# Row tiles move as 64 and 61 rows, and ScalarE's queue issues 19 of the loads between two graph layers

## The reference

```python
def _mgcn_conv(x, edge_index, edge_type, rel, W_in, W_out, W_loop, b, n):
    src, dst = (edge_index[0], edge_index[1])
    m = x[src] * rel[edge_type]
    m = jnp.concatenate([m[:half] @ W_in, m[half:] @ W_out], 0)
    deg = jax.ops.segment_sum(jnp.ones((e,), x.dtype), dst, num_segments=n)
    norm = 1.0 / jnp.maximum(deg, 1.0)
    agg = jax.ops.segment_sum(m * norm[dst][:, None], dst, num_segments=n)
    return jnp.tanh(agg + x @ W_loop + b)
...
h = emb + res * _mgcn_conv(emb, edge_index, edge_type, rel1, W_in1, W_out1, W_loop1, b1, num_nodes)
h = h + res * _mgcn_conv(h, edge_index, edge_type, rel2, W_in2, W_out2, W_loop2, b2, num_nodes)
return h @ mu_w + mu_b
```

## Time and profile before

| | |
|---|---|
| runs before | 1943.16 us median of 3 (1937.86 to 1951.39) |
| the profiled execution | 1951.01 us |
| its span in the trace | 1949.2 us |
| PE busy | 1757.6 us, 90% of the span |
| POOL, DVE, ACT busy | 1300.5, 1223.5, 628.7 us |
| granted TensorE clock, mean | 0.97 |
| queue of SyncE (q1) | 93124 packets, 126.68 MB, 20.2% of 16 engines |
| queue of ScalarE (q10) | 28352 packets, 22.24 MB, 4.2% |

### The profile page before, as it was taken

The page is one execution under the profiler, slowest core; times in us unless marked ns, Lnnn a source line. Parts: engine busy times, 40 slices in busy tenths (PEclk is TensorE's granted clock), DMA queues, the critical chain, the costliest instruction groups (busy, mean ns, idle before and its releaser), DMA issues. The chain is left out here.

```text
span 1949.2 us, 28362 instructions
## 1 busy us (share of the span) xinstructions
PE 1757.6 (90%) x9423; PEld 1294.2 (66%) x9423; DVE 1223.5 (63%) x3583; ACT 628.7 (32%) x1552; POOL 1300.5 (67%) x1297
## 2 busy tenths in 40 slices
PE   2788999998899999989999978987998998988998
PEld 1355867776587777758777645655776676766787
DVE  6777455664756576575556464487665666478766
ACT  4442233343233434333333332231221222222333
POOL 6776777777777777777777733755777676666300
PEclk9999999999899999999999999999999999999999
DMA  9667666667766666776666764667867565555301
GB/s 250 196 200 234 195 207 192 200 191 224 245 197 207 204 193 202 220 248 196 192 203 209 210 192 127 188 197 215 241 192 214 183 202 184 167 176 179 108 14 27
DMA packets 195923, 371.44 MB, mean 191 GB/s; under 512 B 39343, under 2 KB 127445, under 8 KB 195780
## 3 DMA queue, kind: packets, MB, share of 16 engines
q0 software_dynamic: 74304, 220.71, 39.0%
q1 hardware_dynamic: 93124, 126.68, 20.2%
q10 hardware_dynamic: 28352, 22.24, 4.2%
HBM read 305.39 MB, written 64.95 MB: 190 GB/s over the span
## 5 line engine op out<-in xcount | busy, mean ns | idle before, releaser
L1049 POOL DMA_INDIRECT xg<-h_rows,idx_tab x416 | 426.8, 1026 | 205.9 <-issue 125.1
L1049 POOL DMA_INDIRECT xg<-xn_rows,idx_tab x416 | 432.7, 1040 | 141.6 <-issue 123.4
L1001 POOL DMA_INDIRECT rg<-relation_rows,idx_tab x416 | 417.2, 1003 | 136.4 <-issue 126.2
L2880 PE MATMUL ps_hid<-hT,wff 128*128 128x250 f32 (+1 forms) x1920 | 372.3, 347 | 7.0 <-ACT gT L2314 7.0
L2892 PE MATMUL ps_down<-wff,gT 128*125 128x256 f32 x1600 | 366.1, 382 | 0.0
L2880 PEld LDWEIGHTS ps_hid<-hT,wff 128*128 128x128 f32 x1920 | 313.7, 192 | 59.1 <-issue 27.0
L1144 DVE TENSOR_TENSOR xg<-xg,rg 128x256 f32<-128x256 f32 x832 | 296.6, 418 | 71.4 <-DMA xg<-h_rows,idx_tab 40.1
L2892 PEld LDWEIGHTS ps_down<-wff,gT 128*125 128x125 f32 x1600 | 295.4, 189 | 46.3 <-issue 5.1
L2751 PE MATMUL ps_seg<-xg,hot 128*61 128x257 f32 (+1 forms) x1664 | 233.9, 404 | 39.3 <-DVE xg L1144 34.3
L2314 ACT ACTIVATE gT<-ps_hid,b1p 128x250 f32<-128x250 f32 (+1 forms) x480 | 176.8, 434 | 286.6 <-PE ps_hid L2880 286.4
L2751 PEld LDWEIGHTS ps_seg<-xg,hot 128*61 128x61 f32 (+1 forms) x1664 | 103.1, 139 | 134.6 <-issue 67.3
(11 more groups left out here) (382 smaller groups left out, 2420.5 us busy)
## 6 DMA issues: line engine op xcount, KB each, us to landing
second_relation_rows<-rg SPq DMA_DIRECT2D x104, 512.0 KB, 4.0
rg<-second_relation_rows SPq DMA_DIRECT2D x104, 512.0 KB, 4.0
wff<-L_mix_W ACTq DMA_DIRECT2D x8, 1024.0 KB, 7.2
rg<-relation_rows,idx_tab POOLq DMA_INDIRECT x416
xg<-xn_rows,idx_tab POOLq DMA_INDIRECT x416
xg<-h_rows,idx_tab POOLq DMA_INDIRECT x416
h_rows<-qT_all SPq DMA_DIRECT2D x25, 64.0 KB
qrow<-h_rows ACTq DMA_DIRECT2D x25, 64.0 KB
```

What stands on the lines that cost most here:

```text
L1001: pool.indirect_dma_start(rg[:, k, :], None, rel_d, indices(step, 1)).then_inc(s_edge[k // UNIT], 16)
L1049: pool.indirect_dma_start(xg[:, k, 0:D], None, rows, indices(step, 0)).then_inc(s_edge[k // UNIT], 16)
L2880: ins = pe.matmul(hidden, w1[:, c, ff * P:(ff + 1) * P], hT[:, a:z, c, :], start=c == 0, stop=c == KC - 1)
```

## The change

`move_tile` gets pieces of its own, the two strips: 64 and 61 rows in place of 64, 48 and 13. All its users change with it, and the counts that are waited for (16 for each piece) follow. `move_group` keeps the three pieces. The loads of old rows for tiles 6 to 24 leave SyncE's program and go into ScalarE's: there, in the step of tile t, the load for tile t+4 stands behind the column copy of t and the tanh of t-1, and waits for the update of t-2 (`s_hn`). The first six loads stay with SyncE.

```diff
+    TILE_PIECES = STRIPS
...
+        TILE_MOVED = 16 * len(TILE_PIECES)
...
         def move_tile(eng, rows, dram, t, done, store=False):
-            for a, z in PIECES:
+            for a, z in TILE_PIECES:
                 ends = rows[a:z], tile_rows(dram, t, a, z)
                 eng.dma_start(*(ends[::-1] if store else ends)).then_inc(done, 16)
...
             def load_h(t):
-                if t >= AHEAD:
-                    sp.wait_ge(s_hn, t + (1 - AHEAD))
                 move_tile(sp, h_rows[t % AHEAD], xn_d, t, s_hx[t % AHEAD])
...
                     store_relations(stored)
                     stored += 1
-                if t + AHEAD < NT:
-                    load_h(t + AHEAD)
                 store_h1(t)
...
             def dense(f):
+                def load_h(t):
+                    act.wait_ge(s_hn, t + (1 - AHEAD))
+                    move_tile(act, h_rows[t % AHEAD], xn_d, t, s_hx[t % AHEAD])
+
                 def dense_tanh(t):
...
                     if t:
                         dense_tanh(t - 1)
+                    if t > 1 and t - 2 + AHEAD < NT:
+                        load_h(t - 2 + AHEAD)
```

More of the change, by code:

```diff
@@ L492, in build @@
         s_hn = sem("h_new_ready")
-        s_h1 = [counted(f"h1_stored{k}", 16 * len(PIECES)) for k in range(SLOTS)]
+        s_h1 = [counted(f"h1_stored{k}", 16 * len(TILE_PIECES)) for k in range(SLOTS)]
         s_azero = sem("acc_zeroed_again")
@@ L914, in _ @@
             for k in range(SLOTS):
-                sp.wait_ge(s_h1[k], MOVED * (len(range(k, NT, SLOTS)) + 1))
+                sp.wait_ge(s_h1[k], TILE_MOVED * (len(range(k, NT, SLOTS)) + 1))
             def load_relations(u):
@@ L950, in _ @@
                 move_tile(sp, xres[:, t, :], out, t, s_out, store=True)
-            sp.wait_ge(s_out, MOVED * (NG - 1 + GT))
+            sp.wait_ge(s_out, MOVED * (NG - 1) + TILE_MOVED * GT)
         @block.gpsimd
@@ L1038, in _ @@
                     for k in range(SLOTS):
-                        pool.wait_ge(s_h1[k], MOVED * (len(range(k, NT, SLOTS)) + 1))
+                        pool.wait_ge(s_h1[k], TILE_MOVED * (len(range(k, NT, SLOTS)) + 1))
                 for step in range(STEPS2):
@@ L1828, in dense_tile @@
                     dve.wait_ge(s_dy, i + 3)
-                    dve.wait_ge(s_h1[t % SLOTS], MOVED * (t // SLOTS) + MOVED)
+                    dve.wait_ge(s_h1[t % SLOTS], TILE_MOVED * (t // SLOTS) + TILE_MOVED)
                     dve.tensor_tensor(h_new[t % SLOTS], ps_dense[i % 2][0:T, 0:D], bias_of(t), ALU.add).then_inc(s_db, 1)
@@ L2473, in joint @@
                     for k in range(SLOTS):
-                        act.wait_ge(s_h1[k], MOVED * (len(range(k, NT, SLOTS)) + 1))
+                        act.wait_ge(s_h1[k], TILE_MOVED * (len(range(k, NT, SLOTS)) + 1))
                     for t in range(GT):
@@ L3225, in turn_sums @@
                         h = t % AHEAD
-                        pe.wait_ge(s_hx[h], (t - h) // AHEAD * MOVED + MOVED)
+                        pe.wait_ge(s_hx[h], (t - h) // AHEAD * TILE_MOVED + TILE_MOVED)
                         turned = transpose_rows(pe, ps_sums[i % 2][:, KC * T:2 * KC * T], h_rows[h])
@@ L3269, in turn_sums @@
                     h = t % GT
-                    pe.wait_ge(s_hx[h], (dense_loads(h) + t // GT + 1) * MOVED)
+                    pe.wait_ge(s_hx[h], (dense_loads(h) + t // GT + 1) * TILE_MOVED)
                     turned = transpose_rows(pe, ps_x2[:, KC * T:2 * KC * T], qrow[:, h, :])
```

## The result

The changed kernel takes 2027.3 us (median of 4 runs, 2023.4 to 2030.5) against 1944.1 us before (median of 4): a ratio of 1.043, 95% interval 1.038 to 1.047. The time forecast was 2024, with a range of 1980 to 2070. The profiled execution has a span of 2028.8 us, 79.6 more than before.

The account below looks back on a forecast made before the run. SyncE's issuing bound the passage between graph layers; after the change one DMA engine would. Passage +73, joint +5 and end +2.5 us make +80.5: profiled 1951.0 becomes 2031.5, median 1943.2 becomes 2024; range 1980 to 2070.

Parts of the forecast that it names:

- The mechanism: Passage between graph layers: SyncE's issuing binds before; after, 61-row lists of both queues share one DMA engine, 6.44 us a tile.
- faster: Rival, chance 0.09: the 61 rows are dealt out over engines, only issues change, -10 and -2 us: 1931.
- two engines: Rival, chance 0.10: SyncE's and ScalarE's lists run on different engines, no change that shows: 1949.
- Heavier: Rival, chance 0.13: stores at 66 ns a row and ScalarE held, +105, +9 and +3 us: 2060.
- The passage: Stretch between the graph layers: 160.7 us in place of 87.8, +73 us, range +52 to +105.
- The gathers' share: Passage's first stage: 23 gathers put 12.8 us on the one engine that carries the lists.
- The backlog of 7.6 us: Start of the passage: six loads ahead add 15.9 us to the engine, 8.3 free before, 7.6 left over.
- The joint: Before the last layer: ScalarE's five loads in ten issues, held until two lists are left, +5 us (0 to +9).
- The end: Last output store: one issue fewer (0.47 us), but a list of 2.84 us, +2.5 us.
- The pace of 6 to 7 us: Sign: 19 tiles of the passage, those with a load, pass at 6 to 7 us each.
- The last tiles at 3 us: Sign: the passage's last six tiles, with a store alone, pass at 3 us each, 18 us in all.
- ScalarE's load issues would be stretched: Sign: in the passage, ScalarE's load issues take well over 0.5 us each.

Follow-up runs that it names:

- the runs of 59 and 60 rows: Kernel before, tiles moved as 64, 59, 2 or as 64, 60, 1 rows in place of 64, 48, 13: 2022.9 us (1.0383) and 1942.2 us (0.9963).
- the two single lists: Changed kernel with 64 and 61 rows only in the passage's loads, or only its stores, three pieces elsewhere: 1954.8 us (1.0024) and 1968.3 us (1.0115).
- the issues alone: Changed kernel with ScalarE issuing the passage's 19 loads, but every tile in the three pieces of before (64, 48, 13): 1939.0 us, ratio 0.9956.
- the lists alone: Kernel before with pieces of 64 and 61 rows everywhere, SyncE still issuing all the passage's loads: 2024.2 us, ratio 1.0395.
- the passage by itself: Changed kernel with three pieces again in the last layer's loads and the output, 64 and 61 only in the passage: 2009.9 us, ratio 1.0295.

## Why the prediction was right

**The mechanism** stands step by step: SyncE's issuing did bind the passage before (its loads moved away, 10 us of passage go); a list of 61 rows runs on one engine; the lists of both queues share it; and that engine sets the pace. The rivals "faster" and "two engines" fall with the runs of 59 and 60 rows, the packet counts, the two single lists that cost more together than the sum of both, and the rows of both queues in turn on one engine. "Heavier" falls with the pace, 43.3 ns a row and not 66. The Trainium skill, page DMA: Bandwidth & Descriptors, section Issuing engines are not separate DMA queues, says that starting DMAs from several engines saves only the time of issuing, usually small beside the transfer. The runs agree that it is the issuing that is saved, but it was not small here: the issues alone gained 10.3 us of passage and 0.4% of the time. The prediction took 10, as about half of PE's idle time; that it fits so closely is partly luck.

**The sizes** were off in both directions, and the total hides it.
- The passage was forecast at +73 and measured +54.2, at the lower end of its range of +52. Four terms: (1) In the steady stretch seven tiles put 7 x 130 rows of loads and stores and one relation store's 32, 942 rows, on the engine in 40.76 us, 43.3 ns a row if it is never idle, in place of 46.5 (the packets shown above are 42 to 43 apart); and with one relation store in seven tiles in place of five in nineteen, a tile takes 5.82 us in place of 6.44: 12 us less over 19 tiles, 3 of them for relation stores that come back in the second stretch. (2) The gathers' share was about right: the ten tiles of the second stretch take 71.1 us where the steady pace makes 58.2, 12.9 more. Four relation stores are issued in it, where one in seven tiles would make 1.4; the rows of the difference are 3.6 of the 12.9. The other 9.3 are left for the stretch's 19 gathers, for which the forecast's rate makes 10.6 (12.8 for its 23). (3) The backlog of 7.6 us does not show as a term of its own: the first tanh comes 27.6 us after the loads ahead begin, as before (27.3), and the first two tile steps take 2.4 us each, since three slots of `h_new` are free at the start: some 7 us under the steady pace. (4) The last five steps take 4.1 us each (20.65 in all) where 3.0 were forecast, and the gathers start 8.7 us after the last tanh in place of 4.8: the landing of the last list, which the sum had left out. And 4.1 of the 19 us are the marks': from first tanh to first gather the passage before is 91.9, in the forecast, from the first load's issue to the last store's, 87.8.
- The joint was forecast at +5 (0 to +9) and measured +14.6: 11.9 for the ten issues and 2.8 for the three `rg<-x` issues behind them (4.54 us, 1.78 before), which the sum did not have. The step that failed is the pace of the lists beside the gathers. That issuing is held until about two of the five lists are left fits: in the trace's record of packets the third list ends at 1419.0 us, 2.4 after the tenth issue. But three lists took 22.3 us, where the forecast allowed 8.5 to 17, and all five, 325 rows on that engine, 29.5 us (to 1426.2), 91 ns a row, not 46.5.
- The end was forecast at +2.5. From the first output store's issue to the end of the span it is 22.5 us (2006.3 to 2028.8) against 19.9: +2.6. It is 22.5 in the trace of the lists alone as well (1999.3 to 2021.8), and 19.9 where the output goes in three pieces again (1989.8 to 2009.7, the passage by itself).

So +73 and +5 stand against +54.2 and +14.6, 9 us too much. Outside these two stretches the execution was 10.8 us longer, where only the end's 2.5 were forecast, and the other 8 made up for it. The mechanism was right, but that the sum of +80.5 came within 1 us of the measured 79.6 is luck.

**The signs.** Right: two issues a store on SyncE, a DMA share of 0.19 in the steady stretch, and a bias add that waits in 21 of 25 tiles, 4.0 us on average. The pace of 6 to 7 us was a little high (5.8 steady, 7.1 beside the gathers). The last tiles at 3 us were too low (4.1). Wrong: ScalarE's load issues would be stretched. Those rows of the changed kernel (transfer, issues, ns min/median/max, first and last start) show 0.6 us each:

```profile
L790 SPq DMA_DIRECT2D h_rows<-qT_all x50: 428/446/486, 1118.8 to 1255.3; - x50
L790 ACTq DMA_DIRECT2D qrow<-h_rows x50: 223/456/5099, 1396.7 to 1905.5; - x50
L790 ACTq DMA_DIRECT2D qT_all<-xn_rows x26: 477/594/766, 1118.8 to 1233.7; - x26
L790 SPq DMA_DIRECT2D out<-xres x10: 437/458/498, 2006.3 to 2023.8; - x10
...
L790 SPq DMA_DIRECT2D hTa<-xn_rows x2: 438/2386/4335, 1101.8 to 1106.2; - x2
```

ScalarE issues one load a tile there, behind a tanh that waits for the stores, so only about two of its lists are queued at a time (the last load is issued by 1234.4, and the queue's last row starts at 1243.7). Only where lists are issued back to back is the issuer held: 5.1 us for one of the joint's issues, 4.3 for one of SyncE's loads ahead. In the passage the lists hold VectorE, through the slots of `h_new`, and hardly the issuers.

## What to carry to other kernels

Before pieces are merged to save issues, divide the rows of every piece by the numbers from 16 down: the first that divides them is the number of engines the piece gets, as with every cut tried here on SyncE's and ScalarE's queues. The row count on the busiest engine, summed over all queues, then gives the least time of a stage of small transfers; here it was about 43 ns for a row of 1 KB. Fewer issues are worth something only while an issuing engine is the bound; here 64, 60 and 1 rows keep three issues and are at least as fast as before, and two issues with a list of 61 cost 80 us. A term that is small in the sum (a handful of lists at a joint) deserves its own bound when an engine with other work stands behind the issues in its queue.

## What the runs showed of the hardware

- Two queues share an engine row by row: between 1201 and 1205 us SyncE's and ScalarE's rows of 1 KB ran in turn on one engine, 42 to 43 ns apart, 24 GB/s in all, so each queue got half.
- The count of small packets on the page tells on how many engines lists run: one packet of under 512 B for each engine that a list uses, in all the cuts counted.
- An issue of a piece with few rows can be shorter: with 60 and 1 rows SyncE's last seven stores took 16.75 us of issuing, with 48 and 13 it was 17.71, and the shortest single issue 215 ns against 303. By an estimate from these stores, 0.14 us less a tile in 25 stores and 19 loads is 6.0 us, of the 7.1 by which the 60-row cut shortened the passage. This is the likely source of its 0.4%, but it was not tried apart.
- The granted clock averaged 0.75 between 1192.02 and 1232.78, between the levels of 1.2 and 2.4 GHz, where PE was busy for 28.31 of 40.76 us in bursts between its waits. VectorE's waits for stores set the pace there all the same.
